# Squares of the layer 1 logarithms moved from ScalarE to GpSimd in the steady iterations

## What is computed

```python
x = L0_attn_x                              # (32, 256, 128)
xn = _layernorm(x)
x = x + local_and_latent_attention(xn) + clipped_ternary_ffn(xn)     # layer 0
xn = _layernorm(x)
x = x + hyperbolic_attention(xn) + gated_gelu_ffn(xn)                # layer 1
```

```python
neg_inner = einsum(tq, tk) - einsum(sq, sk)
dist = arccosh(maximum(neg_inner, 1.0 + 1e-07))
scores = -dist ** 2 / sqrt(D)
```

## Time and profile before

| | |
|---|---|
| median of three runs | 1960.74 us |
| the profiled execution's own time | 1960.27 us |
| its span, first to last instruction | 1958.5 us |
| PE busy | 1792.7 us (92%) |
| ACT busy | 1679.3 us (86%) |
| DVE busy | 1646.1 us (84%) |
| POOL busy | 1079.7 us (55%) |
| mean granted clock of PE | 0.983 of full speed |

### The profile page before, as it was taken

One profiled execution on the slowest core, in us unless ns is written; L12 is line 12 of the kernel. 1 busy time (PEld: TensorE's weight loads), 2 busy tenths in 40 slices (PEclk: granted clock), 3 DMA queues, 4 the chain that ended last, 5 costly groups with the idle time before them and its releaser, 6 DMA issues.

```text
span 1958.5 us, 51866 instructions
## 1 busy us (share of the span) xinstructions
PE 1792.7 (92%) x17922; PEld 1354.0 (69%) x17922; DVE 1646.1 (84%) x3472; ACT 1679.3 (86%) x2270; POOL 1079.7 (55%) x1208
## 2 busy tenths in 40 slices
PE   4668999999999999999999999999999999999987
PEld 2446777777777777777777777777777777777676
DVE  7788888888888888888888888888888888988884
ACT  8437988889898888989888898988889898887898
POOL 5336655556655555665555666555566655556533
PEclk9778999999999999999999999999999999999999
DMA  7332233233223322323332232333233233323110
GB/s 212 101 90 66 72 90 93 70 70 92 67 70 89 91 70 70 92 64 74 89 91 70 71 90 62 77 89 91 66 75 87 61 81 89 91 62 77 48 47 7
DMA packets 302073, 154.98 MB, mean 79 GB/s; under 512 B 14372, under 2 KB 298052, under 8 KB 302020
## 3 DMA queue, kind: packets, MB, share of 16 engines
q1 hardware_dynamic: 302020, 154.29, 31.4%
HBM read 82.41 MB, written 71.30 MB: 78 GB/s over the span
## 4 chain that ended last, share of the span: by engine, by line
issue 37%; POOL 26%; PE 22%; ACT 7%; DVE 5%; SPq 1%; POOLq 1%; DMA 0%; DVEq 0%; ACTq 0%
POOL zs L1405 11%; PE pu L2260 5%; PE pav L2114 3%; POOL prob L1392 3%; POOL prob L1398 3%; POOL xn L1330 2%; ACT zs L1692 2%; POOL prob L1394 2%; ACT zc L1693 2%; PE pav L2117 1%; PE pm L2235 1%; POOL rs L1313 1%; PE pm L2222 1%; POOL rs L1320 1%; PE pu L2091 1%
## 5 line engine op out<-in xcount | busy, mean ns | idle before, releaser
L1405 POOL TENSOR_TENSOR zs<-zc,zs 128x1024 f32<-128x1024 f32 x192 | 452.3, 2364 | 141.0 <-ACT zc L1693 141.0
L2260 PE MATMUL pu<-hid,h1t 128*128 128x256 f32 x1024 | 252.3, 390 | 0.4 <-DVE nmax L771 0.4
L2260 PE MATMUL pu<-hid,h2t 128*128 128x256 f32 x1024 | 238.5, 381 | 0.0
L1383 POOL TENSOR_TENSOR emb<-xn,w_sur 128x256 f32<-128x256 f32 x32 | 23.5, 733 | 358.2 <-PE pm L2134 358.2
L1692 ACT ACTIVATE zs<-zc,mhalf 128x1024 f32<-128x1024 f32 x192 | 218.7, 1139 | 0.4
L1693 ACT ACTIVATE zc<-zc,phalf 128x1024 f32<-128x1024 f32 x192 | 218.1, 1136 | 0.0
L2260 PEld LDWEIGHTS pu<-hid,h1t 128*128 128x128 f32 x1024 | 185.4, 191 | 40.9 <-issue 20.3
L758 DVE TENSOR_REDUCE zmin<-pu 128x4 f32<-128x1024 f32 (+1 forms) x154 | 187.7, 1219 | 23.9 <-DVE hid L976 16.9
L2260 PEld LDWEIGHTS pu<-hid,h2t 128*128 128x128 f32 x1024 | 187.1, 190 | 22.3 <-issue 0.5
L1713 ACT ACTIVATE zs<-zs 128x1024 f32<-128x1024 f32 x192 | 197.2, 1046 | 2.1 <-POOL zs L1405 2.1
L955 DVE TENSOR_SCALAR zc<-pu 128x1024 f32<-128x1024 f32 x154 | 186.7, 1212 | 0.0
(11 more groups left out here) (316 smaller groups left out, 4752.5 us busy)
## 6 DMA issues: line engine op xcount, KB each, us to landing
scr<-parts SPq DMA_DIRECT2D x256, 192.0 KB, 2.4
q_st<-scr SPq DMA_DIRECT2D x128, 256.0 KB, 3.9
scr<-parts SPq DMA_DIRECT2D x128, 128.0 KB, 2.4
k_st<-scr SPq DMA_DIRECT2D x64, 256.0 KB
k_st<-scr SPq DMA_DIRECT2D x32, 512.0 KB, 5.1
x<-in_L_attn_x SPq DMA_DIRECT2D x32, 128.0 KB, 3.3
out<-xold SPq DMA_DIRECT2D x32, 128.0 KB, 1.8
q_st<-m_t SPq DMA_DIRECT2D x128, 4.0 KB
```

Of the source, the lines that this page charges most:

```text
L1405: G.tensor_tensor(zs[:, c], zc[:, c], zs[:, c], ALU.add).then_inc(sum_done.sem, 1)
L2260: last = PE.matmul(u.ap[:, c * T:(c + 1) * T], w[:, k, c * P:(c + 1) * P], src[:, k, :], start=(k == 0), stop=(k == HC - 1))
```

## The change

`square_log` disappears from ACT and appears on POOL as a product of `zs` with itself. On POOL the six products of an iteration do not stand together: units 0 and 1 come ahead of `attended_input`, unit 2 behind `split0`, unit 3 behind `residual1`, unit 4 behind `residual0`, unit 5 behind `values_mid`. The closing part is as before.

```diff
--- before.py
+++ after.py
@@ -1404,6 +1404,12 @@
                 pool.wait_ge(sqrt_done.sem, sqrt_done.at(l, n + 1))
                 G.tensor_tensor(zs[:, c], zc[:, c], zs[:, c], ALU.add).then_inc(sum_done.sem, 1)
 
+            def square_log(l, n):
+
+                c = slice(n * UNIT, (n + 1) * UNIT)
+                pool.wait_ge(ln_done.sem, ln_done.at(l, n + 1))
+                G.tensor_tensor(zs[:, c], zs[:, c], zs[:, c], ALU.mult).then_inc(sq_done.sem, 1)
+
             def sum_minima(l):
 
                 pool.wait_ge(zsr_ready.sem, zsr_ready.at(l))
@@ -1445,18 +1451,28 @@
                 if run.quantise:
                     clip_first(m)
                 if e:
+                    square_log(e, 0)
+                    square_log(e, 1)
                     attended_input(run, e)
                 if f:
                     split0(f, link[F])
+                if e:
+                    square_log(e, 2)
                 if l:
                     residual1(run, l)
+                if e:
+                    square_log(e, 3)
                 if f:
                     clip_input(run, f)
                     residual0(run, f)
+                if e:
+                    square_log(e, 4)
                 if m:
                     power(rs1, ve1, var1, rstd1, m)
                 if l:
                     values_mid(run, l)
+                if e:
+                    square_log(e, 5)
                 if m:
                     importance_products(run, m)
                 if l:
@@ -1712,12 +1728,6 @@
                 act.wait_ge(sum_done.sem, sum_done.at(l, n + 1))
                 S.activation(zs[:, c], zs[:, c], ACT.Ln).then_inc(ln_done.sem, 1)
 
-            def square_log(l, n):
-
-                c = slice(n * UNIT, (n + 1) * UNIT)
-                act.wait_ge(ln_done.sem, ln_done.at(l, n + 1))
-                S.activation(zs[:, c], zs[:, c], ACT.Square).then_inc(sq_done.sem, 1)
-
             def weights1(run, n):
 
                 u = unit(run, f"sub{n}")
@@ -1764,26 +1774,19 @@
                     log(e, 1)
                     shift_part(run, "mT1", 1)
                     log(e, 2)
-                    square_log(e, 0)
                 if m:
                     gate_exp(m)
                 if e:
                     log(e, 3)
-                    square_log(e, 1)
                 if m:
                     copied(misc(run, "mixT"), out_t[:], misc(run, "mixT").ap[:, 0:T])
                 if e:
-                    square_log(e, 2)
                     log(e, 4)
                     log(e, 5)
-                    square_log(e, 3)
                     weights1(run, 0)
                     copied(unit(run, "f3"), hid3[:].rearrange("p c t -> p (c t)"), unit(run, "f3").ap)
                 if m:
                     copied(misc(run, "x1T"), xn1_t[:], misc(run, "x1T").ap[:, 0:T])
-                if e:
-                    square_log(e, 4)
-                    square_log(e, 5)
                 if l:
                     importance_exp(l)
                 if e:
```

## The result

The changed kernel takes 2194.41 us (median of four runs, 2191.76 to 2197.04), the kernel before beside it 1961.07 us. The ratio is 1.1185, with a 95% interval of 1.1171 to 1.1198. That is 233 us more, 8.3 us in each of the 28 iterations. The forecast was 2263 us with a range of 2125 to 2340 us: the direction and the range held, and both mechanisms that it names (POOL's order and the turns) are there, but the size was 69 us too large, and the last part shows that this is a sum of errors of both signs.

What follows compares the result with a forecast made beforehand. PE was taken to set the pace, with 2.6 us idle per 57 us iteration. 9.1 us of lateness plus 1.7 us of clock, 10.8 us over 28 iterations, adds 302 us to 1960.27: 2263 us, range 2125 to 2340.

Steps and rivals of the forecast that it cites:

- the turns: DVE's instructions with all tiles in SBUF and POOL's wait for each other; raises PE's lateness from 5.7 to 9.1 us.
- PE sets the pace, ACT's shorter list wins nothing: Whole iteration: PE busy 54.4 of 57 us; six squares fewer on ACT, 6.3 us, costed at zero.
- The sum, 9.1 + 1.7 = 10.8 us: Per iteration: PE's transpose of xn1 9.1 us late plus 1.7 us for PE's clock; 28 iterations 302 us.
- rival 3: Unit 5 gets between the two instructions of normed1 (L731): 13.1 us an iteration, 2327 us; chance 0.20.
- The price of a product, 2.36 us: Each POOL product priced like POOL's sum of the same shape, 2.364 us; six are 14.2 us an iteration.
- The mix is 2.5 us late, and this is absorbed by what follows: DVE's gate and mix, in turns with POOL, end at 940.1 instead of 937.44; PE waits 2.5 us, absorbed later.
- L880 7.2 us late: DVE's L880 starts at 947.0, after L776 waits for unit 2, L942 for x1res and L944 for unit 3.
- rival 2: Only turns that a row shows; L944 and L731 go free: 8.5 us an iteration with the clock, 2198 us; chance 0.20.
- The power and the pair L731: Unit 4 ahead of POOL's power, which ends at 951.9; normed1 (L731) ends at 952.9 instead of 943.55, 9.35 us late.
- The clock, 1.7 us an iteration: After PE's waits, 3.3 us of dense work at half clock in each iteration, costing 1.7 us.
- Queue order only, 5.7 us an iteration: Rival 1: turns cost little, POOL's list order alone delays PE 5.7 us, 7.4 with the clock; 2167 us; chance 0.15.

Runs made afterwards that it cites:

- fillers at the first wait alone: The changed kernel with 28 more transposes of a constant on PE in front of the mix's transposes; 2248.49 us.
- places of 1.97 us and nothing read: Against the kernel before: all squares stay on ACT, POOL clears unread small tiles with memsets at the changed kernel's six places; 2077.40 us, ratio 1.0590.
- nothing late: The changed kernel with units 0 to 3 moved directly behind the residual x1res and units 4 and 5 behind normed1; 2200.81 us.

## Why the prediction was right, and where it was wrong

*PE sets the pace, ACT's shorter list wins nothing.* Right: the kernel with one product moved off ACT's list for free is at 0.9996, and in the changed kernel, with six moved off, PE's waits for ACT kept their size.

*The sum, 9.1 + 1.7 = 10.8 us.* Measured: 8.3 us. PE's transpose of `xn1` was 8.0 us late in place of 9.1, and the clock added 0.3 us to that in place of 1.7. That the range held is partly luck, since errors offset each other: L880 came 2.2 us less late than forecast, while unit 5 inside L731, which the forecast had left to rival 3, added 1.6 us.

*The price of a product, 2.36 us.* Wrong: it takes 1.89 us. The nearest row had the same shape but two different tiles as operands. With different operands in three units the kernel takes 2269 us, 6 us from the forecast, and its period is the forecast 68 us. There the clock's term is right as well (L901 waits 1.7 us in every iteration), but three units are still short and unit 5 is still inside L731, so the nearness is partly luck.

*The mix is 2.5 us late, and this is absorbed by what follows.* It was 3.7 us late, and nothing absorbed it: it is the largest row of the table. The walk had L857 wait for unit 1 alone; it stood behind the first step of `split0`, so all that follows came later, and L872 met unit 2. This is not the product's length: with 2.36 us for units 0 to 2, L872 met unit 2 too and the mix was later still. In the sum it was counted all the same, since the 7.2 us of L880 were taken from DVE's list behind the mix.

*L880 7.2 us late.* It was 5.0. L776 met unit 3, L942 and L944 met nobody (L944 is at 0.23 us), and so DVE waited for POOL once behind the mix and not three times. Whether L944 would take a turn is left open by this trace, but L893, of the same kind (a scalar from a pointer), does (1.95 us). So the condition of rival 2 was false although its number, 2198 us, is the nearest.

*The power and the pair L731.* The product ahead of the power counted as said. Rival 3's turn, unit 5 inside L731, happened in every steady iteration; it was worth 2.0 us an iteration, 1.6 of them its own, and I had given it a chance of 0.20.

*The clock, 1.7 us an iteration.* The fall came in every iteration, at full value for PE, but behind the first wait, where DVE's chain covers it and it costs 0.2 us. I placed it behind the second wait. There it came in every fifth iteration only, and then cost 1.6 us, near my price. The kernel with fillers at the first wait alone, where it falls behind the second, loses 2.2 us an iteration by it.

*Queue order only, 5.7 us an iteration.* With places of 1.97 us and nothing read, order costs 3.8 us and the clock 0.3; with nothing late, the turns cost 7.3 us and the clock 1.3. The two do not add: each fills part of the other's wait.

## What to carry to other kernels

An engine at 55% is not free: ask at which moments it idles, who waits for the results behind the new work in its list, and whether the other engine of a shared port runs short instructions beside it. A 0.2 us instruction of DVE between SBUF tiles takes at least as long as what is left of the POOL instruction that it meets, so long POOL work belongs beside DVE work that reads PSUM or reduces. A stall of PE is priced where it lies, and its clock's fall with it: removing one stall can carry the fall to a place where it costs more. One iteration of the trace is not all of them: here each fifth was 1.6 us longer, and the periods of all iterations, read in a row, settle what the walk through one leaves over.

## What I had not expected of the hardware

- On POOL a two-operand instruction whose operands are one tile takes 1.892 us for 128 x 1024, with two tiles 2.364 us, in multiplication and addition alike.
- Between two instructions of one DVE line that follow each other at once, a waiting POOL product gets in: the pair of L731 went from 0.59 to 2.19 us.
- A DVE instruction that waits for POOL is not always next: L857 took 2.02 us, from under unit 1 to the end of the second POOL instruction behind it.
- Memsets on POOL did not hold the last instruction of the mix, which has two SBUF inputs (0.43 us at most beside memsets, 0.83 in the changed kernel).
- PE ran at 0.56 of full clock over 6.6 us of dense work after a wait of 3.65 us, and at 1.00 throughout when the waits were filled with work.
- After the same wait of 2.07 us, in one kernel, the clock fell in three iterations of four and stayed at 1.00 in the fourth.
